# Attention on one core: transposed probabilities replaced by key-major scores with a shift that is spread through DRAM

## The reference

```python
def _L0_xattn_ref(hidden_states, audio_kv, audio_attention_mask, Wq, Wk, Wv, Wo, ln_gamma, ln_beta, gate):
    a = _layer_norm(audio_kv, ln_gamma, ln_beta)
    Q = (hidden_states @ Wq.T).reshape(B, Tt, HEADS, HEAD_DIM).transpose(0, 2, 1, 3)
    K = (a @ Wk.T).reshape(B, Ta, HEADS, HEAD_DIM).transpose(0, 2, 1, 3)
    V = (a @ Wv.T).reshape(B, Ta, HEADS, HEAD_DIM).transpose(0, 2, 1, 3)
    scores = jnp.einsum('bhtd,bhsd->bhts', Q, K) * scale
    scores = jnp.where(mask, scores, jnp.float32(-jnp.inf))
    attn = jax.nn.softmax(scores, axis=-1)
    out = jnp.einsum('bhts,bhsd->bhtd', attn, V)
    out = out.transpose(0, 2, 1, 3).reshape(B, Tt, D) @ Wo.T
    return hidden_states + jnp.tanh(gate) * out
...
x = _L0_xattn_ref(x, ctx_2048, mask_BxS2_bf1, ...)
x = _L1_xattn_ref(x, ctx_2048, ...)
```

## Time and profile before

| | us |
|---|---|
| median of 3 runs | 1564.92 (1564.41 to 1566.0) |
| the profiled execution | 1566.05 |
| its span | 1564.0 |
| TensorE busy | 1417.6 (91% of the span) |
| VectorE busy | 924.6 (59%) |
| ACT busy | 719.6 (46%) |
| Pool busy | 469.6 (30%) |
| mean granted TensorE clock | 0.957 |

### The profile page before, as it was taken

The page is one execution under the profiler, slowest core; times in us unless marked ns, Lnnn a source line. Parts: engine busy times, 40 slices in busy tenths (PEclk is TensorE's granted clock), DMA queues, the critical chain, the costliest instruction groups (busy, mean ns, idle before and its releaser), DMA issues. The chain is left out here.

```text
span 1564.0 us, 41370 instructions
## 1 busy us (share of the span) xinstructions
PE 1417.6 (91%) x16448; PEld 1015.8 (65%) x16448; DVE 924.6 (59%) x2287; ACT 719.6 (46%) x1772; POOL 469.6 (30%) x530
## 2 busy tenths in 40 slices
PE   4999999999999999568799999998998999999965
PEld 3777777777777777356475656564756575657522
DVE  2444444444444443337777887778777878887651
ACT  3666666666666666422443334333433443334312
POOL 1211111111111111124333543353335324533330
PEclk9999999999999999877999999999999999999977
DMA  7531111111111100020000001000000000000000
GB/s 202 148 87 39 39 39 37 37 37 37 37 37 37 37 13 13 18 116 12 19 26 19 9 24 26 25 3 24 25 19 8 25 26 19 8 25 20 19 7 12
DMA packets 25695, 55.12 MB, mean 35 GB/s; under 512 B 3984, under 2 KB 6672, under 8 KB 24016
## 3 DMA queue, kind: packets, MB, share of 16 engines
q1 hardware_dynamic: 25552, 52.99, 11.9%
HBM read 42.23 MB, written 7.34 MB: 32 GB/s over the span
## 5 line engine op out<-in xcount | busy, mean ns | idle before, releaser
L899 POOL TENSOR_TENSOR rst<-rp,st 128x448 f32<-128x448 f32 x192 | 194.6, 1037 | 73.5 <-DVE st L1095 73.5
L269 POOL TENSOR_TENSOR aT_lo<-whole,aT_hi 128x375 fp32r<-128x375 f32 x64 | 58.7, 917 | 445.1 <-ACT whole L421 442.3
L891 POOL TENSOR_TENSOR xm<-mixed,xa 128x448 f32<-128x448 f32 x80 | 85.3, 1081 | 299.4 <-DVE mixed L1024 262.0
L341 DVE CUSTOM_DVE_ANT_0 probs<-a_bank,unmask 112x375 f32<-112x375 f32 x256 | 126.0, 545 | 79.6 <-PE a_bank L538 72.4
L440 ACT ACTIVATE probs<-probs,least 112x375 f32<-112x375 f32 x256 | 153.8, 608 | 0.0
L347 DVE RECIPROCAL inv_rows<-sums 112x128 f32<-112x128 f32 x64 | 61.0, 953 | 155.8 <-ACT probs L440 155.8
L449 ACT COPY probsT<-a_bank 125x448 f32<-125x448 f32 x192 | 90.1, 536 | 51.7 <-PE a_bank L593 51.7
L1103 DVE TENSOR_TENSOR rst<-rp,st 128x448 f32<-128x448 f32 x64 | 111.7, 1747 | 0.0
L593 PEld LDWEIGHTS a_bank<-ident_sb,probs 112*125 112x125 f32 x768 | 90.8, 188 | 31.1 <-ACT keyT L431 16.3
L1599 PE MATMUL b_bank<-rst,b_collect 128*32 128x448 f32 x512 | 68.5, 606 | 37.5 <-DVE rst L1103 36.6
L593 PE MATMUL a_bank<-ident_sb,probs 112*125 112x112 f32 x768 | 99.3, 279 | 3.4 <-ACT probs L440 3.4
(11 more groups left out here) (167 smaller groups left out, 3139.2 us busy)
## 6 DMA issues: line engine op xcount, KB each, us to landing
ctx_tok<-in_ctx SPq DMA_DIRECT2D x16, 750.0 KB
xT_sb<-in_xT SPq DMA_DIRECT2D x16, 224.0 KB, 9.7
x_tok<-in_x SPq DMA_DIRECT2D x16, 224.0 KB, 9.4
x_between_layers<-x_sb SPq DMA_DIRECT2D x16, 224.0 KB, 2.3
b_x<-x_between_layers SPq DMA_DIRECT2D x16, 224.0 KB, 2.8
x_post<-x_between_layers SPq DMA_DIRECT2D x16, 224.0 KB, 2.8
out_dram<-fin SPq DMA_DIRECT2D x16, 224.0 KB, 2.3
vbd<-vtok SPq DMA_DIRECT2D x208, 16.0 KB
```

The lines of the kernel that those rows point to most:

```text
L341: dve.tensor_tensor_reduce(out=probs[:, g % 2, i], in0=score_bank[i][0:T, 0:TC], in1=unmask[:, m[1]], scale=-SCALE, scalar=-LOWEST, op0=AL ...
L891: pool.tensor_tensor(xm[:, f % 2], mixed[:, f % 2], xa[:, :, 1:T + 1], ALU.add).then_inc(s_xm, 1)
L899: pool.tensor_tensor(by_chunk(rst[:, j % NPROD]), by_chunk(rp[:].rearrange("p c t -> p (c t)")), state_of(j), ALU.mult).then_inc(s_pprod, 1)
```

## The change

Row-major scores are still made, masked and put through exp, but now only for the least value and the sum of each row. From these a shift is made per row and head, `shift = least − log(sums)`, 112 x 16 values (`logs` on ACT, `row_shift` on VectorE). Two groups of heads at a time it is turned on TensorE (`turn_shift`, units S0 and S1), copied, stored to DRAM and read back so that each of 125 partitions has the whole row (`spread_shift` on SP). The scores are then made a second time, with keys on the partitions: `key_major_scores`, 12 matmuls of 32 x 125 by 112 a group into the same four score banks. VectorE scales them and adds the shift (`shift_scores`, 125 x 448, three a group), and ACT takes exp with the key's mask as bias (`exps_key_major`, three a group), which gives the normalised probabilities as `weigh_values` needs them. `transpose_probs`, `copy_probsT`, `invert_sums`, `spread_inv`, `copy_inv` and the multiplication in `scale_attn` go.

The steps are put in another order: row-major scores of batch n are made in step n, directly behind its keys; context transposes, their copies and splits and the query projections of batch n+1 in step n; those of batch 0 ahead of `run`. A second mask, with keys on the partitions, is loaded by a DMA of one-byte elements (125 x 16 x 3) and expanded once. Loads run two batches ahead, the weights of the second layer are issued one a step, and its constants at step 14 rather than 3.

```diff
-RING = ["T0", "T1", "T2", "T3", "q0", "q1", "P00", "P01", "P02", "K0", "K1", "P10", "P11", "P12", "K2", "I0", "K3",
-        "P20", "P21", "P22", "V0", "V1", "P30", "P31", "P32", "V2", "I1"]
-RING_FIRST = [u for u in RING if u[0] in "TqKV"]
-RING_LAST = [u for u in RING if u[0] in "PI"]
+RING = ["K0", "S1", "K1", "K2", "qa", "K3", "V0", "S0", "V1", "V2", "T0", "T1", "T2", "T3", "qb"]
+RING_START = ["T0", "T1", "T2", "T3", "qa", "qb"]
+RING_FIRST = [u for u in RING if u != "S1"]
+RING_NEXT_LAST = [u for u in RING if u[0] not in "Tq"]
...
+            def spread_shift(b, half):
+                sp.wait_ge(s_ringev, unit_done(later(b, half), f"S{half}"))
+                sp.dma_start(shift_rows_in_dram(half).rearrange("g (i t) -> (g i) t", t=T), shift_T[:, half]).then_inc(s_shift_out, 16)
+                sp.wait_ge(s_shift_out, 16 * count(b, 2, half + 1))
+                sp.dma_start(shift_cols[:, 2 * half:2 * half + 2],
+                             shift_rows_in_dram(half).rearrange("(o g) f -> o g f", o=1).broadcast_to([TK, 2, HG * T])).then_inc(s_shift_in[half], 16)
...
+            sp.dma_start(key_mask8[:], A["mask"].rearrange("b (k p) -> p b k", p=TK),
+                         allow_slow_non_contiguous=True).then_inc(s_w["key_mask"], 16)
...
-                    load_ctx(later(n, 1))
-                    load_x(later(n, 1))
+                m, l = later(n, -1), later(n, -2)
+                if normalise and not is_batch(n, B - 2):
+                    load_x(later(n, 2))
                 if attend:
-                    load_xtok(later(n, -1))
-                if is_batch(n, 1):
+                    spread_shift(m, 1)
+                if finish:
+                    store_x1(l)
+                if attend:
+                    load_xtok(m)
+                if normalise and not is_batch(n, B - 2):
+                    load_ctx(later(n, 2))
+                if project:
+                    spread_shift(n, 0)
...
                 if project:
-                    split_aT(n)
+                    take_key_mask(n)
                 if normalise:
+                    mask_to_inf(later(n, 1))
                     rsqrt(later(n, 1))
-                if project:
-                    mask_to_inf(n)
+                    split_aT(later(n, 1))
 
             pool.wait_ge(s_const, 1)
             rsqrt((0, 0))
+            mask_to_inf((0, 0))
+            split_aT((0, 0))
+            key_masks_to_inf()
             run(pool, step)
...
+            def row_shift(b, half):
+                dve.wait_ge(s_log, count(b, 2, half + 1))
+                if at_least(b, 1):
+                    dve.wait_ge(s_ring, unit_done(later(b, half - 1), f"S{half}"))
+                dve.tensor_tensor(shift[:, 2 * half:2 * half + 2], least[:, 2 * half:2 * half + 2], log_sums[:, 2 * half:2 * half + 2],
+                                  ALU.subtract).then_inc(s_shift, 1)
+            def shift_scores(m, g):
+                if g % 2 == 0:
+                    dve.wait_ge(s_shift_in[g // 2], 16 * count(m, 1, 1))
+                if g >= 2 or at_least(m, 1):
+                    dve.wait_ge(s_av, count(m, C, g - 1))
+                dve.wait_ge(s_scoreT, count(m, C, g + 1))
+                for k in range(KT):
+                    dve.scalar_tensor_tensor(out=probsT[:, g % 2, k].rearrange("p (i t) -> p i t", t=T), in0=score_bank[0:TK, :, k * T:(k + 1) * T],
+                                             scalar=SCALE, in1=shift_cols[:, g].rearrange("p (i t) -> p i t", t=T),
+                                             op0=ALU.mult, op1=ALU.add).then_inc(s_shifted, 1)
...
+                    shift_scores(m, 0)
                 if finish:
                     residual(l)
                 if attend:
-                    mask_scores(m, 1, range(HG))
+                    row_shift(m, 1)
+                if project:
+                    mask_scores(n, 0, range(HG))
+                if attend:
+                    shift_scores(m, 1)
+                if project:
+                    mask_scores(n, 1, range(HG))
+                if attend:
+                    copy_attn(m, 0)
+                    shift_scores(m, 2)
+                if normalise:
+                    ln_stats(later(n, 1))
+                if project:
+                    row_shift(n, 0)
+                    mask_scores(n, 2, range(HG))
                 if normalise:
                     ln_apply(later(n, 1))
...
+            def logs(b, half):
+                act.wait_ge(s_exp, count(b, HEADS, (2 * half + 2) * HG))
+                if at_least(b, 1):
+                    act.wait_ge(s_shift, count(later(b, -1), 2, half + 1))
+                act.activation(log_sums[:, 2 * half:2 * half + 2], sums[:, 2 * half:2 * half + 2], ACT.Ln).then_inc(s_log, 1)
+
+            def copy_shift(b, half):
+                n = later(b, half)
+                act.wait_ge(s_ring, unit_done(n, f"S{half}"))
+                if at_least(b, 1):
+                    act.wait_ge(s_shifted, count(later(b, -1), C * KT, (2 * half + 2) * KT))
+                act.copy(shift_T[:, half], unit_bank(n, f"S{half}")[0:2 * HG, 0:T]).then_inc(s_ringev, 1)
+
+            def exps_key_major(m, g):
+                if g == 0:
+                    act.wait_ge(s_kmask, count(m, 1, C + 1))
                 for k in range(KT):
...
+                    act.activation(probsT[:, g % 2, k], probsT[:, g % 2, k], ACT.Exp, bias=key_mask[:, m[1], k:k + 1]).then_inc(s_expT, 1)
...
-                    exps(m, 1, (0, 1))
+                    logs(m, 1)
+                    exps_key_major(m, 0)
                 if project:
                     copy_key(n, 0)
                 if attend:
-                    exps(m, 1, (2, 3))
+                    copy_shift(m, 1)
+                if is_batch(n, 0):
+                    round_weight(W["wv"], wv_hi, "wv")
+                    exps(n, 0, (0, 1))
                     copy_key(n, 1)
+                    exps(n, 0, (2, 3))
                 if attend:
-                    copy_probsT(m, 1)
-                    exps(m, 2, (0, 1))
+                    exps_key_major(m, 1)
                 if project:
                     copy_key(n, 2)
+                    if normalise:
+                        copy_query(later(n, 1), "a", slice(0, 2))
+                    exps(n, 1, range(HG))
+                    copy_key(n, 3)
+                    logs(n, 0)
                 if attend:
...
+                    exps_key_major(m, 2)
                 if project:
                     copy_value(n, 0)
-                if attend:
-                    exps(m, 3, (2, 3))
-                if project:
+                    copy_shift(n, 0)
+                    exps(n, 2, range(HG))
                     copy_value(n, 1)
...
-            def scores(m, g):
-                if g == 0:
-                    pe.wait_ge(s_ringev, unit_done(m, "K3"))
-                if g > 0 or at_least(m, 1):
-                    pe.wait_ge(s_masked, count(m, HEADS, g * HG))
+            def scores(b, g):
+                pe.wait_ge(s_ringev, unit_done(b, f"K{g}"))
+                if at_least(b, 1):
...
+            def key_major_scores(m, g):
+                if is_batch(m, B - 1):
...
+                    pe.wait_ge(s_masked, count(later(m, 1), HEADS, g * HG))
...
-                        pe.wait_ge(s_exp, count(m, HEADS, (g + 1) * HG))
                     for i in range(HG):
+                        rows = slice(i * HD, (i + 1) * HD)
+                        last = pe.matmul(score_bank[0:TK, i, k * T:(k + 1) * T], keyT[rows, m[1], g, k * TK:(k + 1) * TK],
+                                         query[rows, m[1], g], start=True, stop=True)
+                last.then_inc(s_scoreT, 1)
...
+            def turn_shift(b, half):
+                dst = free_unit(later(b, half), f"S{half}")
+                pe.wait_ge(s_shift, count(b, 2, half + 1))
+                pe.transpose(dst[0:2 * HG, 0:T], shift[:, 2 * half:2 * half + 2].rearrange("t g i -> t (g i)"), ident[0:T, 0:T]).then_inc(s_ring, 1)
...
                 if finish:
                     project_out(l)
-                    project_query(n, 1)
                 if attend:
-                    scores(m, 1)
-                    transpose_probs(m, 0)
+                    key_major_scores(m, 0)
                 if project:
                     project_key(n, 0)
+                    scores(n, 0)
                 if attend:
-                    weigh_values(m, 0)
+                    turn_shift(m, 1)
                 if project:
                     project_key(n, 1)
                 if attend:
-                    scores(m, 2)
-                    transpose_probs(m, 1)
+                    weigh_values(m, 0)
+                    key_major_scores(m, 1)
                 if project:
                     project_key(n, 2)
+                if normalise:
+                    project_query(later(n, 1), "a", (0, 1))
+                if project:
+                    scores(n, 1)
+                    project_key(n, 3)
```

(40 more changed lines are left out.)

273 lines of the change are left out of this document (124 added, 149 removed).

## The result

The changed kernel takes 1620.57 us (median of 4 runs, 1615.81 to 1622.47), the kernel before on the same chip 1565.46 (4 runs, 1564.41 to 1567.28): a ratio of 1.0347, 95% interval 1.0326 to 1.0369. It is slower by 55 us, where 26 were forecast: the direction is right and the time lies inside the stated range of 1562 to 1642, but less than half of the slowdown was foreseen. All medians and ratios here are of fast runs: one run of e5_shift_first (3380.95 us) and one of the kernel before beside it (1790.22) were slow and are left out.

What follows compares the result with a forecast made beforehand. TensorE was taken to bound the attention, busy all the time. Head +14.5, work −46, waits +51, key mask +7 and tail −1 gave +25.5: 1592 us, slower by 1.6%, range 1562 to 1642.

Steps and rivals of the forecast that it cites:

- (a): Head of the attention: Pool takes the mask ahead of batch 0's splits, so K0 starts later; +14.5 us.
- (b): TensorE's work per batch: transposes and spread_inv gone, key-major groups and turns added; −2.9 a batch, −46 us.
- R2: Rival: key-major matmuls on TensorE run one behind the other, 2.6 a group; +113 us, 1705; chance .05.
- w3: TensorE: the third context transpose after V2 waits for V2's bank; .2, 15 times, +3 us.
- (c): New waits in TensorE's row, w1, w2 and w3 together; +51 us.
- w1: TensorE: scores(n,0) waits for ACT's copy of K0; 1.2 a loop step, +24 us in all.
- w2: TensorE: turn_shift(n,0) waits for row_shift(n,0), behind other work on VectorE; 1.6 a step, +24 us.
- (d): Key mask's DMA of 6000 one-byte runs: between hidden and landing 12 late for Pool; +7 us.
- R4: Rival: one-byte DMA runs cost .05 to .11 us, key mask holds batch 1; 1621 to 1693; chance .09.
- R5: Rival: the shifts' way through DRAM is late; +30 us, 1622, if 2 us late; chance .08.
- R3: Rival: ACT empties its pipeline behind table switches, two a batch on the path; +38 us, 1630; chance .04.
- R1: Rival, faster: VectorE and ACT run ahead, only K0's copy is waited for; −22 us, 1544; chance .12.

Runs made afterwards that it cites:

- e5_shift_first: e3 with row_shift(n,0) moved ahead of shift_scores(m,2) and the context's statistics on VectorE; 1583.21 us.
- e7: e3 with Pool splitting the transposed context of batch 0 before it takes the mask at the start; 1592.68 us.
- e6: e3 with copy_key(n,0) moved ahead of exps_key_major(m,0) on ACT; 1574.64 us.
- e9: e3 with the logarithm of the row sums replaced by the identity function, so ACT needs no other table; 1584.63 us.
- e8: The edits of e3, e5_shift_first, e6 and e7 together on the changed kernel; 1552.83 us, ratio .9938 to the kernel before.
- e1: The changed kernel with the attention's loop written out, no jump back; 1633.45 us.
- e4: The kernel before with 22 unread matmuls of 8 columns added a step, lengthening its loop; 1695.94 us.
- e2: The kernel before with the attention's loop written out, as a control; 1565.43 us.
- e3: The changed kernel with the attention's query projection in 16 matmuls of 128 weight columns instead of 32 of 64, loop kept; 1601.05 us.

## Why the prediction was right or wrong

The steps of the prediction, one by one:

(a) The head was right: K0 at 41.90 for the predicted 43.7 (the mask landed 15.7 after its issue instead of 17.8), and e7 moves the first project_out back by 14.7.

(b) TensorE's own work was mis-sized: −46, measured −29. The key-major group took .85, as estimated from the row-major group, and the turns less than thought, .03 and .19; R2 is out. What was removed, though, was 5.33 a batch, group by group from 287.41 on (1.38, 1.33, 1.33, 1.29), and 5.48 in the next, not 5.6: the prediction had taken the mean of two groups for all four. And nearly every other kind of group became a little longer in its new place: out 3.62 for 3.52, queries 3.43 for 3.22, keys 9.11 for 8.97, values 8.92 for 8.79, transposes of the context 1.78 for 1.44 (w3, .3 for the forecast .2). These sum to .9 a batch; the prediction had priced moved groups at their old duration. Why they are longer was not tried.

(c) w1 and w2 were right in place, cause and size, 45.4 for 48, and each fell when only its cause was moved (e5, e6) while the other stayed (23.4 and 22.6). In size w2 was helped a little by the tail: it is 1.3 to 1.4 in a loop step for the 1.6 forecast, and 2.73 in the last. That the written-out steps have a longer w1 came from the order of ACT, and e9 shows the table load in it. What the prediction did not have is the clock behind a wait of 2.1.

(d) The key mask had landed by 43.8, near the lower end (46), and was hidden, so the 7 us of this term were nothing; R4 is out. R5 too: VectorE's additions wait for the shift's transfer once, for 1.9 us, and otherwise for TensorE.

The step that failed is the unwritten one: that the loop costs at its jumps what it cost before, nothing. "(b) TensorE's work per batch" counted the passes of the new group, 24 for 12, for their time alone. As instructions they carried the loop past what stays resident: 14.3 us idle and 8.8 of slow clock. The attention came out 34 us above its forecast (59.3 for 25.5). The jumps are 23 of these, (b) with w3 is 14 (−29 for −43) and the slow clock behind the waits of 2.1 about 5; the head, the key mask and the two waits were together 11 cheaper than forecast, and about 3 is the remainder. That the time still lies in the stated range is luck: its upper part had been priced for a late key mask, R3, R5 and one more wait, and none of these came.

R1's deciding point of 2.2 us of wait a batch was put too high, as the work saved is 29 and not 46: (29 + 1 − 14.5)/15 = 1.0. w1 and w2 were 3.0 a batch, above either. In e8 the attention ends 6.6 us ahead of the kernel before; without the 10.2 of the head it would end about 4 behind, which is an estimate from e7, and was not run.

## What to carry to other kernels

Count the instructions of a hardware loop as a resource of its own: passes and weight loads of each turn, of TensorE above all. While the trace shows no instruction packets in the loop, ask how far the change is from that limit, and if it crosses it, look for instructions that do little (two narrow matmuls for one wide one) before writing the loop out. Compare runs by the stretch that was changed as well as by the total, since a stretch that nobody touched can differ by 20 us between two kernels (e1). And where a transfer, a split or a copy is put ahead of others in an engine's row, price what queues behind it: three moved lines were worth 48 us here (1601 to 1553), which turned a loss into a gain.

## What the runs showed of the hardware

- A turn of 1408, 1448 and 1504 passes and weight loads on TensorE is run without loading instructions; one of 1576 or 1584 loads 9 packets of 16 KB in each turn and stalls behind the jump for 3.3 to 4.0 us (the change) or twice 1.5 to 2.0 (e4). Written-out code takes 6 or 7 packets in 84 us (e1, e2) and has no such stall. Why the loop loads more than straight code was not tried.
- TensorE's granted clock went down after idle times of 3.3 to 4.0 us (project_out of 6.41 or 5.38 for 3.69) and after some of 2.1 (matmuls of .52 for .33, up to 1.5 us more in that step), not after those of 1.1 to 1.4 in the loop. In e4 it went down with no idle time at all, behind 22 passes of 8 columns (.50 from 160 to 165).
- A DMA of 6000 runs of one byte, issued at 18.1 us behind a load of 656 KB, had landed by 43.8.
- A matmul of 8 columns with 112 x 128 weights took .22 us in two passes (e4, 11 in 2.39 from 322.41 on), where one of 112 columns with 128 x 128 weights took .23 (e3, 8 in 1.87): here few columns saved next to nothing.
- A table load on ACT took 1.28 us, and the activation behind it started 1.29 to 1.30 after the load did (402.50 to 403.80, 404.03 to 405.32).
